# Second attention of a two-layer gated block: where the second six products of a row block's queries and outputs stand in an odd step

## The reference, cut to what matters

```python
q = _ln((x @ Wq + bq).reshape(b, s1, H, HD), qn_w, qn_b)       # x after a layer norm
k, v = _ln(y_main @ Wk + bk), y_main @ Wv + bv                 # 240 rows of context
k_dca, v_dca = _ln(...), ...                                   # the 16 rows left
ctx = softmax(q @ k.T * SCALE) @ v + softmax(q @ k_dca.T * SCALE) @ v_dca
x = x + tanh(g) * (ctx @ Wo + bo)
```

## Time and profile before

| | |
|---|---|
| median of three runs | 3544.81 us |
| the profiled execution | 3546.12 us, its span 3544.4 us |
| TensorE busy | 3464.4 us (98% of the span) |
| VectorE busy | 2313.4 us (65%) |
| ScalarE busy | 1866.7 us (53%) |
| GpSimd busy | 1339.6 us (38%) |
| mean granted TensorE clock | 0.989 |
| second attention, 2184 to 2868 us | 128 steps of a pair of heads and some at both ends |

### The profile page before, as it was taken

How to read it: one execution, slowest core, us unless ns; L and a number is a source line. 1 busy time by engine, 2 the same in 40 slices (tenths; PEclk the granted TensorE clock), 3 DMA queues, 4 the chain that set the end, 5 groups by cost and what they waited for, 6 DMA issues and landing times. The chain is left out here.

```text
span 3544.4 us, 66282 instructions
## 1 busy us (share of the span) xinstructions
PE 3464.4 (98%) x22490; PEld 3000.9 (85%) x22490; DVE 2313.4 (65%) x5703; ACT 1866.7 (53%) x4822; POOL 1339.6 (38%) x1345
## 2 busy tenths in 40 slices
PE   9999999999999999899999998899999989999999
PEld 8999999999999999799999996667777668888887
DVE  6666666656666666576767778787777754545543
ACT  5555555554444444455555554787777743333332
POOL 3222222332333322254544554777777640202020
PEclk9999999999999999899999999999999999999999
DMA  4566666535666665577767764222222245344341
GB/s 166 188 237 236 236 238 237 167 98 189 236 236 233 230 235 167 184 272 251 261 250 261 259 247 143 68 89 67 64 70 64 73 128 160 110 129 126 112 131 48
DMA packets 430862, 611.00 MB, mean 172 GB/s; under 512 B 95120, under 2 KB 226320, under 8 KB 426512
## 3 DMA queue, kind: packets, MB, share of 16 engines
q1 hardware_dynamic: 330128, 394.91, 34.1%
q10 hardware_dynamic: 90208, 179.32, 13.7%
q0 software_dynamic: 10272, 33.63, 2.8%
HBM read 339.34 MB, written 268.44 MB: 171 GB/s over the span
## 5 line engine op out<-in xcount | busy, mean ns | idle before, releaser
L853 POOL TENSOR_TENSOR a_prob<-a_prob,a_rinv 128x512 f32<-128x512 f32 x256 | 266.4, 1041 | 1005.2 <-DVE a_rinv L1071 1005.2
L773 ACT ACTIVATE a_prob<-a_prob,a_low_bias 128x256 f32<-128x256 f32 x512 | 256.5, 502 | 469.7 <-DVE a_low_bias L1062 468.2
L527 PE MATMUL a_pj<-a_xt,in_hi 128*128 128x256 f32 x1024 | 309.8, 302 | 0.1
L1378 POOL TENSOR_TENSOR e_act_hi<-e_act_f,e_zeros 128x256 fp32r<-128x256 f32 x128 | 181.5, 1418 | 308.0 <-DVE e_act_f L1608 308.0
L1392 PE MATMUL e_gb<-e_xt_hi,in_hi 128*128 128x256 f32 x1024 | 291.7, 285 | 1.4 <-DVE e_xt_lo L1587 1.4
L1393 PE MATMUL e_gb<-e_xt_lo,in_hi 128*128 128x256 f32 x1024 | 290.9, 284 | 0.0
L1394 PE MATMUL e_gb<-e_xt_hi,in_lo 128*128 128x256 f32 x1024 | 290.9, 284 | 0.0
L2997 DVE TENSOR_TENSOR raw_in<-turned,raw_in 128x512 f32<-128x512 f32 x224 | 151.9, 690 | 212.5 <-PE turned L2710 209.6
L529 PE MATMUL a_pj<-a_xt,in_lo 128*128 128x256 f32 x1024 | 289.0, 282 | 0.0
L528 PE MATMUL a_pj<-a_xt,in_hi 128*128 128x256 f32 x1024 | 288.8, 282 | 0.0
L901 DVE TENSOR_TENSOR a_ot_lo<-a_avb,a_ot_hi 128x256 fp32r<-128x256 f32 x256 | 108.4, 423 | 258.2 <-ACT a_ot_hi L782 258.0
(11 more groups left out here) (478 smaller groups left out, 11299.3 us busy)
## 6 DMA issues: line engine op xcount, KB each, us to landing
raw_in<-in_w_gate SPq DMA_DIRECT2D x39, 2048.0 KB, 8.2
x_sorted<-a_spare ACTq DMA_DIRECT2D x42, 1792.0 KB
y_sorted<-a_spare ACTq DMA_DIRECT2D x42, 1792.0 KB
raw_out<-in_w_out SPq DMA_DIRECT2D x40, 1024.0 KB
in_hi<-w_ops SPq DMA_DIRECT2D x224, 128.0 KB, 2.3
in_lo<-w_ops SPq DMA_DIRECT2D x224, 128.0 KB, 2.4
raw_in<-in_x SPq DMA_DIRECT2D x32, 512.0 KB, 6.1
xt_rows<-a_xt SPq DMA_DIRECT2D x16, 1024.0 KB, 5.9
```

The source lines that it names most:

```text
L527: nc.tensor.matmul(out, a_hi, b_hi, start=start, stop=False)
L773: e = nc.scalar.activation(prob[:, u % 4, t], prob[:, u % 4, t], ACT.Exp, bias=low_bias[:, u % 2, t:t + 1], scale=-1.0, accum_out=rsum[:, ...
L853: nc.gpsimd.tensor_tensor(prob[:, u % 4], prob[:, u % 4], rinv[:, u % 2].unsqueeze(2).to_broadcast([P, 2, S]), ALU.mult).then_inc(p_done, 1)
```

## The change

In the table of pieces, the steps -7 and 13, both odd, no longer have six products of `q1` or `o1` at `early` and six at `late`. All twelve stand at `late`, in two entries behind each other. The steps of `q0` and `o0`, which are even, are left as they are.

```diff
-        for n, a, b in ((-10, ("k0", 0), None), (-9, ("k1", 0), None), (-8, ("q0", 0), ("q0", 1)), (-7, ("q1", 0), ("q1", 1)), (-6, None, ("v1", 0)),
-                        (-5, ("v0", 0), None), (12, ("o0", 0), ("o0", 1)), (13, ("o1", 0), ("o1", 1))):
+        for n, a, b in ((-10, ("k0", 0), None), (-9, ("k1", 0), None), (-8, ("q0", 0), ("q0", 1)), (-7, None, ("q1", 0)), (-7, None, ("q1", 1)), (-6, None, ("v1", 0)),
+                        (-5, ("v0", 0), None), (12, ("o0", 0), ("o0", 1)), (13, None, ("o1", 0)), (13, None, ("o1", 1))):
             if a:
                 plan(n, "early", *a)
             if b:
```

## The result

| | before | after |
|---|---|---|
| median, first measurement | 3542.65 us (3538.79 to 3544.84, 4 runs) | 3567.92 us (3567.26 to 3569.39, 4 runs) |
| ratio, 95% interval | | 1.0070 (1.0057 to 1.0082) |
| second measurement, on another occasion | 3540.28 us (9 runs) | 3568.86 us (5 runs), ratio 1.0076 (1.0063 to 1.0090) |
| the profiled execution | 3546.12 us | 3567.36 us |

The change makes the kernel 25.3 us slower in the first measurement and 28.6 in the second. Predicted were 27.9 us, to 3572.7, with a range of 3560 to 3585. The intervals are 20 to 29 us and 22 to 32. Two executions stood far off in a slow state, 4991.1 us of the kernel before and 6854.2 of the one with `q1` alone; the ratios leave them out, and they move the medians that count them by at most 0.3 us.

The account below looks back on a forecast made before the run. TensorE's order was taken to bound the kernel. 27.3 us for 29 steps, plus 1.4 for batch 1, less 0.8 coming back, made 27.9 us on the median of 3544.8: 3572.7 us, range 3560 to 3585.

Parts of the forecast that it names:

- The sum of the waits: TensorE's waits for other engines over the whole second attention, put at 36.0 us.
- The fixed cost of a piece: Pieces of products between TensorE's transposes: joining two gains 0, at most 0.1 us a site.
- The new wait: In `q1` and `o1` steps, transposes wait for ScalarE's copy of `ptb`; each step grows by 0.94 us.
- the ends (0 and 1.21): Bounds on a site's cost in us: no wait for the copy, or the trace's back-to-back groups 1.65 apart.
- rival (a), late copies: At the changed steps, the copy shifts into ScalarE's exponentials: 1.21 us a site, 35.7 in all, 3580.5 us; chance 0.12.
- How often: Second attention: 15 sites of `o1` and 14 of `q1`, 29 x 0.94 = 27.3 us.
- batch 1's 1.4 us: Batch 1's `q1` step: transposes can't start earlier, so the six moved products cost all of their 1.38 us.
- four returns of 0.22: Step behind `o1` in four batches with keys made earlier: wait for GpSimd's scaling covered, 4 x 0.2 = 0.8 us back.
- (b): Second attention: earlier scores let half of TensorE's 36 us of waits go, 10.7 us slower, 3555.5 us; chance 0.09.
- (c): Second attention: the head start at 29 sites empties all 36.0 us of waits, 3537.5 us, faster by 0.2%; chance 0.03.
- (e), no cost: At the changed steps, the copy wait is hidden or the products were already adjacent: 3544.8 + 1.4 us; chance 0.05.
- (d), the clock: TensorE's clock falls in the batches with made keys: 5 us a batch, 20 in all, 3592.7 us; chance 0.04.

Follow-up runs that it names:

- `q1` alone: Only the `q1` entry changed as in the change, `o1` left in two pieces of six, against the kernel before: 3555.55 us against 3543.89, ratio 1.0034.
- The cut at three: Kernel before with both blocks cut 3 and 9, three products ahead of the transposes and nine behind the scores: 3552.20 us against 3543.89, ratio 1.0022.
- the longer copy: 32 of ScalarE's copies preceded by an extra half-bank copy: kernel before 3541.10 us against 3540.22, ratio 1.0002; changed kernel 3575.59, ratio 1.0098.
- a second bank: Changed kernel with the first group of transposes in the projection bank in the 29 steps: 3544.74 us against 3540.22 before, ratio 1.0013.
- the unused bank: Kernel before with three of eight transpose groups in the unused projection bank, in the four batches with made keys: 3542.92 us against 3540.22, ratio 1.0007.
- all twelve at the head: Kernel before with all twelve products of `q1` and `o1` ahead of the step's first transposes: 3555.06 us against 3543.89, ratio 1.0039.

## Why the prediction was right

*What bounds the kernel.* That TensorE's order is the time held: the 0.94 us that the change puts into a step show in full at the end of the stretch, but for returns of 0.22 us and less. The sum of the waits was put at 36.0 us; TensorE's list for the window has one more, 0.7 us, which changes nothing.

*The fixed cost of a piece* was put at nothing. The steps confirm it: 6.29 us against 6.28 worked out with no gain from joining.

*The new wait* was predicted at 0.94 us a step and measured at 0.93 to 0.95. The transposes stand 1.36 us apart, 1.38 predicted. The choice between the ends (0 and 1.21) rested on ScalarE's idle time ahead of the copy, and the copy does start when the transposes end. The cut at three gave the same 1.36 with other work between, and the longer copy moved it by its own 0.28. So rival (a), late copies, is out.

*The Trainium skill's rule* ("Perfetto Trace Analysis", Matmuls) that groups should rotate through banks so that evacuation lies under the next products was weighed as the one that speaks against the change. This case agrees with it: with a second bank 4.5 us of the loss are left. The attempt with the unused bank shows its limit here, since turning through another bank gained nothing where GpSimd was next.

*How often.* 29 steps, batch 1's 1.4 us (TensorE waited 1.2 for VectorE's take of `q0`) and four returns of 0.22 are all in the trace. The small return of 0.05 to 0.1 in each of the other batches was not in the sum, and makes up the 0.9 us between 27.9 and 27.0. Why it is there wasn't followed.

*The rivals.* Waits coming back (b) and (c): the other kinds of wait stayed within 0.1 us, but for the scaling's. (e), no cost: out. (d), the clock, didn't happen in the changed kernel. It did happen once each in two experiments, at 4.4 and 2.9 us, both times in a stretch of transposes, scores and values alone, as (d) has it; 5 us a batch was its price. The 20 us that were put on it, all four batches at once, were never seen.

*What was not foreseen.* The margin between kernels includes the clock at the start and the end of the second attention, 2.6 and 2.5 us here. That the difference of the medians came to 25.3 once and to 28.6 once, on either side of the 27.0 in the trace, is chance as far as the runs tell. It makes the difference of two profiled executions (21.2) a poor measure of the change; the copies between the two ends are a better one.

## What to carry to other kernels

A piece of work between two uses of one buffer isn't filler: its length is the cover for whoever empties the buffer, and only what exceeds the need (here 1.82 - 1.38 = 0.44 us) can be taken away. To price such a move, take the distance that the emptying engine needs, from its start to the next use, and look whether that engine is idle when its input comes. Where an order was moved the other way, look at the in-order engine behind it, as with all twelve at the head: what it has queued behind the instruction that now waits is late as well.

## What the runs showed of the hardware that was not expected

TensorE's granted clock fell to the lower level for 10.3 us in the middle of the steady part of one execution (all twelve at the head), in a stretch without a product of the projections. The same execution has six more such stretches, 14.4 to 15.1 us long from product to product, all at 1.00. In a second kernel with the same order, in the same place, it stayed at 1.00 too. In the kernel before, the seven stretches are 11.3 to 13.0 us long and at 1.00 (the earlier trace rows has a part of the last). So a stretch that keeps the clock in one batch can lose it in the next; what decides it isn't shown.
